# Two causal self attentions: the query projection moves behind the second scores, the value projection in front of the values product

## The reference

```python
def _L1_attn_ref(x, W, b):                    # the first has w_proj, b_proj behind it
    B, T, C = x.shape; H = 16; D = C // H     # H = 16 heads of D = 16
    qkv = jnp.einsum('btc,oc->bto', x, W) + b
    q, k, v = jnp.split(qkv, 3, axis=-1)      # each to (B, H, T, D)
    att = jnp.einsum('bhtd,bhsd->bhts', q, k) / math.sqrt(D)
    att = jax.nn.softmax(jnp.where(causal, att, -jnp.inf), axis=-1)
    y = jnp.einsum('bhts,bhsd->bhtd', att, v)
    return y.transpose(0, 2, 1, 3).reshape(B, T, C)
```

## Time and profile before

| what | value |
|---|---|
| three runs, median (lowest to highest) | 1419.83 us (1418.65 to 1424.13) |
| the profiled execution | 1422.47 us |
| its span, first to last instruction | 1420.7 us |
| mean granted TensorE clock | 0.966 of full |
| busy: PE, PE weight loads, DVE, ACT, POOL | 91%, 71%, 58%, 47%, 39% |
| layer 2 self attention | about 318 to 459 us |
| layer 5 self attention | about 680 to 812 us |

### The profile page before, as it was taken

How to read it: one execution, slowest core, us unless ns; L and a number is a source line. 1 busy time by engine, 2 the same in 40 slices (tenths; PEclk the granted TensorE clock), 3 DMA queues, 4 the chain that set the end, 5 groups by cost and what they waited for, 6 DMA issues and landing times. The chain is left out here.

```text
span 1420.7 us, 30900 instructions
## 1 busy us (share of the span) xinstructions
PE 1295.5 (91%) x9938; PEld 1008.4 (71%) x9938; DVE 822.8 (58%) x1838; ACT 668.3 (47%) x1386; POOL 558.5 (39%) x763
## 2 busy tenths in 40 slices
PE   6999999989997675999788689999999999999998
PEld 5777777767775343777666457888888788888886
DVE  4666666656775885455688776444444444444443
ACT  4655555534453786554344353343343344343333
POOL 2233333346775333222577643333323232333332
PEclk9999999979999897999999899999999999999999
DMA  8100000000000000110000003333333253333331
GB/s 271 41 16 15 15 15 7 1 1 2 0 0 0 1 0 21 40 43 15 2 0 0 23 24 122 104 117 114 103 112 114 76 163 112 103 118 114 103 111 63
DMA packets 34038, 81.84 MB, mean 58 GB/s; under 512 B 4356, under 2 KB 11524, under 8 KB 33992
## 3 DMA queue, kind: packets, MB, share of 16 engines
q1 hardware_dynamic: 32952, 80.21, 17.5%
q10 hardware_dynamic: 1040, 1.05, 0.2%
HBM read 78.87 MB, written 2.38 MB: 57 GB/s over the span
## 5 line engine op out<-in xcount | busy, mean ns | idle before, releaser
L2096 POOL TENSOR_TENSOR sw<-sg,wb 128x512 f32<-128x512 f32 x136 | 176.6, 1299 | 398.4 <-ACT sg L1995 383.3
L2050 DVE TENSOR_TENSOR a<-sw,ps 128x512 f32<-128x512 f32 x136 | 93.6, 688 | 234.7 <-POOL sw L2096 234.6
L2000 ACT ACTIVATE ah<-a 128x512 fp32r<-128x512 f32 x136 | 86.0, 633 | 289.3 <-DVE a L2050 280.4
L1923 PE MATMUL ps<-Hh,wh 128*128 128x512 f32 x544 | 215.9, 397 | 3.2 <-DVE wl L2036 2.7
L1925 PE MATMUL ps<-Hh,wl 128*128 128x512 f32 x544 | 213.8, 393 | 0.0
L1924 PE MATMUL ps<-Hl,wh 128*128 128x512 f32 x544 | 213.0, 392 | 0.0
L626 ACT ACTIVATE Pr<-ps,mx 128x256 f32<-128x256 f32 x256 | 107.7, 496 | 116.7 <-DVE mx L528 116.5
L2054 DVE TENSOR_TENSOR al<-a,ah 128x512 fp32r<-128x512 f32 x136 | 94.2, 693 | 62.1 <-ACT ah L2000 58.6
L534 DVE COPY PT<-ps 128x512 f32<-128x512 f32 x128 | 88.4, 691 | 68.1 <-PE ps L393 68.1
L1923 PEld LDWEIGHTS ps<-Hh,wh 128*128 128x128 f32 x544 | 102.5, 188 | 26.0 <-issue 4.2
L1925 PEld LDWEIGHTS ps<-Hh,wl 128*128 128x128 f32 x544 | 102.7, 189 | 24.2
(11 more groups left out here) (219 smaller groups left out, 2671.6 us busy)
## 6 DMA issues: line engine op xcount, KB each, us to landing
wb<-token_weights SPq DMA_DIRECT2D x66, 512.0 KB, 3.6
raw<-in_ew SPq DMA_DIRECT2D x68, 384.0 KB, 3.1
cx<-in_ctxT SPq DMA_DIRECT2D x32, 256.0 KB, 2.7
X<-in_x SPq DMA_DIRECT2D x1, 1536.0 KB, 7.3
wqkv<-in_wqkv SPq DMA_DIRECT2D x2, 768.0 KB, 5.9
raw3g<-in_wg SPq DMA_DIRECT2D x1, 1024.0 KB, 5.4
raw3u<-in_wu SPq DMA_DIRECT2D x1, 1024.0 KB, 7.4
raw3d<-in_wd SPq DMA_DIRECT2D x1, 1024.0 KB, 9.6
```

The lines of the kernel that those rows point to most:

```text
L1923: eng.matmul(ps[:, bank, :], wh[:, u, w], HhT[:, c, cols], start=(c == 0), stop=False)
L2000: eng.activation(ah[:, tt, :], a[:, tt, :], ACT.Copy).then_inc(m_ah, 1)
L2050: eng.tensor_tensor(a[:, tt, :], sw[:, tt, :], ps[:, UB[tt], :], ALU.mult).then_inc(m_a, 1)
L2096: eng.tensor_tensor(sw[:, tt, :], sg[:, tt, :], wb[:, u, tt * UT:(tt + 1) * UT], ALU.mult).then_inc(m_sw, 1)
```

## The change

Both self attentions. On PE, `qkproj` is split in two: `kproj` stays in its place, `qproj` goes behind the second scores, and `vproj` goes behind the first transposes, in front of the layernorm's transposes and the values product. The semaphore of the projection, `a_qk`, counts two steps a pair instead of one, and `qproj` waits until ACT has copied both halves of K (`a_ke`), since K and Q share a bank. On ACT, the copy of K goes in front of the first exp, that of Q stays behind it. On DVE, `mask(i, 1)` goes in front of `normalise`, `next_mean` and `ln_dve2`. POOL's code is untouched.

```diff
--- before.py
+++ after.py
@@ -821,7 +821,7 @@
     OB, OW = 4, 2 * HD + 2
     FV, FQ, FB = 5, 6, 7
 
-    per_pair = {"qk": 1, "ke": 2, "qe": 2, "kbd": 4, "v": 1, "ve": 4, "s": 2, "m": 2, "max": 2, "sub": 2, "exp": 2, "t": 2,
+    per_pair = {"qk": 2, "ke": 2, "qe": 2, "kbd": 4, "v": 1, "ve": 4, "s": 2, "m": 2, "max": 2, "sub": 2, "exp": 2, "t": 2,
                 "te": 2, "pv": 2, "rd": 1, "on": 1, "t2": 1, "t2e": 1, "wo": 1, "xb": 1}
 
     def counter(name, credit=0, by=None):
@@ -879,10 +879,18 @@
                                          start=True, stop=True, tile_position=(0, SEQ * b))
                 ins.then_inc(a_pv, 1)
 
-            def qkproj(i, u):
+            def kproj(i, u):
                 eng.wait_ge(ln_hT, g["lnt"][L] + i + 1)
                 eng.wait_ge(a_qe, given(a_qe) + 2 * i)
-                for m in (2, 3, 0, 1):
+                for m in (2, 3):
+                    for c in range(2):
+                        ins = eng.matmul(ps[:, FQ, m * P:(m + 1) * P], w[:, c, m * P:(m + 1) * P],
+                                         hT[:, u, c, :], start=(c == 0), stop=(c == 1))
+                ins.then_inc(a_qk, 1)
+
+            def qproj(i, u):
+                eng.wait_ge(a_ke, given(a_ke) + 2 * i + 2)
+                for m in (0, 1):
                     for c in range(2):
                         ins = eng.matmul(ps[:, FQ, m * P:(m + 1) * P], w[:, c, m * P:(m + 1) * P],
                                          hT[:, u, c, :], start=(c == 0), stop=(c == 1))
@@ -916,15 +924,17 @@
                 if opening(i):
                     ln_pe(eng, L, 0, 0, FH)
                 if front:
-                    qkproj(i + 1, v)
+                    kproj(i + 1, v)
                 if tail:
                     pv(i - 1, v, 1)
                 if mid:
                     scores(i, u, 1)
                 if front:
+                    qproj(i + 1, v)
+                if mid:
+                    turn(i, u, 0)
+                if front:
                     vproj(i + 1, v)
-                if mid:
-                    turn(i, u, 0)
                 if tail and proj:
                     tail2(i - 1, v)
                 if further(i):
@@ -1018,6 +1028,8 @@
                     ln_dve(eng, L, i + 2, u)
                 elif closing(i) and proj:
                     ln_dve(eng, L + 1, 0, v)
+                if mid:
+                    mask(i, 1)
                 if tail:
                     normalise(i - 1, v)
                 if late and not proj:
@@ -1026,8 +1038,6 @@
                     ln_dve2(eng, L, i + 2, u)
                 elif closing(i) and proj:
                     ln_dve2(eng, L + 1, 0, v)
-                if mid:
-                    mask(i, 1)
                 if late and not proj:
                     next_keep(i - 2, u)
                 if front:
@@ -1049,12 +1059,15 @@
                 eng.wait_ge(a_pv, given(a_pv) + 2 * (i - 1) + k + 1)
                 eng.activation(PT[:, k, :, :], ps[:, TB, :], ACT.Copy).then_inc(a_te, 1)
 
-            def qk_out(i, u):
-                eng.wait_ge(a_qk, given(a_qk) + i + 1)
+            def k_out(i, u):
+                eng.wait_ge(a_qk, given(a_qk) + 2 * i + 1)
                 eng.wait_ge(a_kbd, given(a_kbd) + 4 * (i - 1))
                 for m in range(2):
                     eng.activation(KT[:, u, m, :], ps[:, FQ, (2 + m) * P:(3 + m) * P], ACT.Identity,
                                    bias=bqk[:, 2 + m:3 + m]).then_inc(a_ke, 1)
+
+            def q_out(i, u):
+                eng.wait_ge(a_qk, given(a_qk) + 2 * i + 2)
                 eng.wait_ge(a_s, given(a_s) + 2 * (i - 1))
                 for m in range(2):
                     eng.activation(Qs[:, u, m, :], ps[:, FQ, m * P:(m + 1) * P], ACT.Identity,
@@ -1071,10 +1084,12 @@
                     turned(i - 1, 1)
                 if opening(i):
                     ln_act(eng, L, 0, 0, FH)
+                if front:
+                    k_out(i + 1, v)
                 if mid:
                     exps(i, 0)
                 if front:
-                    qk_out(i + 1, v)
+                    q_out(i + 1, v)
                 if mid:
                     turned(i, 0)
                 if tail and proj:
```

More of the change, by code:

```diff
@@ L924, in body @@
                 if front:
-                    vproj(i + 1, v)
+                    qproj(i + 1, v)
                 if mid:
                     turn(i, u, 0)
+                if front:
+                    vproj(i + 1, v)
                 if tail and proj:
```

## The result

| | before | after |
|---|---|---|
| median of the runs (lowest to highest) | 1420.29 us (1418.65 to 1424.13) | 1433.69 us (1431.09 to 1435.71) |
| ratio, with its 95% interval | | 1.0086 (1.0065 to 1.0108) |
| span of the profiled execution | 1420.7 us | 1431.8 us |
| mean granted TensorE clock | 0.966 | 0.959 |

A forecast was written before the change was run, and what follows sets the result against it. Bounds: PE's own work in layer 2, a ring of waits through several engines in layer 5. Layer 2 +3.0 and layer 5 +2.5 make +5.5 us, from 1419.83 to 1425.3; range 1415 to 1430, the forecast's own 1422 to 1429.

The forecast's parts named there:

- Layer 2's loop: Layer 2's twelve loop passes: h loses the port contest to POOL's subtraction, PE waits, about +0.3 us a pass, +3.6 us.
- The dead heat: Layer 2: DVE's h (5.34 us) and POOL's second subtraction (5.33) start together after the first scores; subtraction taken to be first.
- Rival (a): Layer 2: h comes ahead of POOL's subtraction, -0.39 us a pass; layer 5 as forecast; whole kernel 1417.0 us; chance 0.32.
- Layer 5's loop: Layer 5's loop passes: ring of waits grows from 7.70 to 7.85 us, +0.15 a pass, +1.8 us over twelve rings.
- ring: Layer 5: chain of waits through several engines from one pair's second mask to the next pair's, forecast at 7.85 us.
- the first leg: Layer 5: second mask to POOL's second subtraction, now behind nmv, neps and rs: 3.22 us instead of 1.48, +1.74.
- Rival (b): Layer 5: POOL's neps stands behind all of DVE's h, ring up to 0.25 us longer, +3.3; kernel 1428.6 us; chance 0.12.
- Rival (c): Layer 5: POOL's detour is off the path, DVE's work bounds at some 7.2 us, and (a) holds; 1406.5 us; chance 0.06.
- The last passes of layer 2: Last two passes of layer 2: no h transposes to wait for, mask ahead of a wait for lnrs, -0.8 us.
- Layer 5's end: End of layer 5: long leg paid without the savings, +1.0 us for pair 14 to 15 and +1.7 behind the last mask.
- The first two pairs of layer 5: Layer 5, pairs 0 and 1: no next_scale yet, PE's own work and h bind at about 7 us, -2.0 for both.
- Openings: Layer 2's opening pass: query projection waits an estimated 0.7 us for K's copies, mostly swallowed by the first exp, +0.2 us.

## Why the prediction was wrong

**Layer 2's loop: right.** The forecast was a pass of 8.46, 3.6 us over twelve passes at 0.3 each; measured 8.46 and 4.06. Counted from the first scores (401.03), forecast to measured: second scores 2.65 to 2.67, mask 3.38 to 3.40, reciprocal 4.70 to 4.73, h 5.34 to 5.35, subtraction 5.33 to 5.15, h's end 6.52 to 6.34, next pass 8.46 to 8.42. The dead heat was a clear win for POOL by 0.20, because lnrs and Kbd ran 0.1 to 0.18 sooner than I chained them. That the pass still came out right is in part luck: h's transposes started at 6.40 and not at 6.59, but from them to the next pass lie 2.02 and not 1.87, and the two errors nearly cancel. Rival (a) would have needed h 0.2 sooner, not the 0.02 to 0.1 I gave it: its chance of 0.32 was too high. The run in which the subtraction waits for h shows about what (a) would have been worth: 7.86 a pass, not 7.75.

**Layer 5's loop: right.** The legs, forecast to measured: mask to subtraction 3.22 to 3.25, subtraction to transposes 1.76 to 1.76, transposes to values product 1.45 to 1.48, to the next mask 1.32 to 1.32; ring 7.85 to 7.81, +1.8 to +1.95. (The terms given for the first leg add up to 3.20, not 3.22, which changes nothing.) Rival (b), neps behind all of h, did not come: neps takes 0.27 beside h against 0.19 in other places, and from neps to the subtraction lie 0.96, as before (0.97). neps does end 0.05 after h (759.87 and 759.82), so it may well have stood behind h's last 0.2; the price was what the old row already held. Rival (c) was excluded by the order, as argued.

**The last passes of layer 2: wrong in sign. This is the step that failed.** It read: "the last two passes have no h transposes to wait for, and the mask stands ahead of a wait for lnrs: -0.8." Measured +2.23. The mask is indeed earlier (0.73 after its scores instead of 1.88), but I followed only the mask. On PE the transposes of the last softmax stand behind On's transposes and the output projection of the pair before, and On is exactly what the mask was moved ahead of. So PE waits 0.82 longer, and at this point the clock falls: +1.13. The run with the old mask order at the ends gives -2.8 for this end. The wait for On is shown by it; that the clock falls because of the wait is not, since it also fell once without it.

**Other terms.** Layer 5's end +2.7 forecast, +2.99 measured. The first two pairs of layer 5 -2.0 forecast, -0.94 measured: those passes fell to 7.17 each. The -2.0 was wrong by itself: from the 15.27 us of the kernel before, two passes at the "about 7" that I gave save 1.3, not 2.0. Openings +0.2 forecast, +0.1 measured in sum; the wait of 0.7 for K's copy is there as forecast.

**The account.** By the profiles +11.1 against +5.5, a miss of 5.6: layer 2's end +3.0, first pairs +1.1, both loops +0.6, untouched code +0.7, the rest +0.2. By the medians the change moved 13.4, 2.3 more than by the profiles, and the median before rose by 0.5 with more runs; together 8.4, the distance from 1425.3 to 1433.69. Of the 2.3, 2.2 come from the choice of the execution: the one profiled before took 1422.47, 2.2 above the median of 1420.29, and the one profiled after (1433.60) was at its median. The chance of slower, 0.29, was too low because the range held only the uncertainty of the loops (and their bounds add up to 1422.3 to 1427.9, not to the 1429 that I gave); I gave the ends single values without bounds, and the ends made half of the loss.

## What to carry to other kernels

Chaining an operation's start on each engine through one pass, from rows, gave ring lengths to 0.05 us; do the same for the written-out first and last passes, which have other pieces and so another chain, and give them bounds of their own. When a step is moved ahead, list everything that now stands behind it and ask of each who waits for it: here it was h in one layer, the scale in the other, and On at the end. A change made of two parts should be priced apart: PE's order alone gained 0.7%, and the accompanying move on DVE, on top of it, cost 1.6%.

## What the runs showed of the hardware

- A DVE h of 0.40 us takes 0.99 beside a POOL subtraction of 1.04, 0.82 when it starts later in it, 0.62 to 0.73 beside Kbd. The subtraction itself shows 1.04 to 1.09 there.
- PE's clock level matters at the ends of these pipelined loops. The same output projection takes 1.13 or 2.07 us. Behind the early mask, which adds a wait of 0.8 us, it was 2.07 in all eight kernels; behind the old order it was 1.13 in five of six and 2.07 in one. What else decides it stays open.
- In the kernel with only the mask's move, layer 5's ring ran at full clock for a while (PE busy 12.4 of 16 us from 760 to 776) and at a mix of both levels later: 8.7 against 10.2 to 10.4 us a pass. What makes the clock fall within such a loop stays open.
